# A graph layer's tiles with a second accumulator, another order of TensorE's work, and VectorE's loop over gathered pairs behind pair 2

## The reference

```python
def _graph_conv_max(x, src, dst, W_rel, b, W_root):          # N = 1250 nodes, 41250 edges, D = 512
    agg = jax.ops.segment_max(x[src], dst, num_segments=N)
    agg = jnp.where(jnp.isfinite(agg), agg, 0.0)
    return agg @ W_rel.T + b + x @ W_root.T
h = jax.nn.relu(_graph_conv_max(layernorm(x), src, dst, W1_rel, b1, W1_root))
h = jax.nn.relu(_graph_conv_max(h, src, dst, W2_rel, b2, W2_root))
x = x + h
x = x + experts(layernorm(x))                                # router, top 512 of each of 8 experts, gelu, sum
```

## Time and profile before

| | us |
|---|---|
| median of 3 runs | 1025.27 (1024.95 to 1028.95) |
| span of the profiled execution | 1025.1 |
| tiles 1 to 9 of layer 0, from end of `agg` to end of `agg` | 286.9 |
| tiles 11 to 19 of layer 1 | 297.6 |
| DVE busy in these | 212.0 and 232.7 |
| PE busy in these | 212.5 and 228.4 |

### The profile page before, as it was taken

How to read it: one execution, slowest core, us unless ns; L and a number is a source line. 1 busy time by engine, 2 the same in 40 slices (tenths; PEclk the granted TensorE clock), 3 DMA queues, 4 the chain that set the end, 5 groups by cost and what they waited for, 6 DMA issues and landing times.

```text
span 1025.1 us, 9702 instructions
## 1 busy us (share of the span) xinstructions
PE 726.0 (71%) x2541; PEld 329.5 (32%) x2541; DVE 681.6 (66%) x1232; ACT 270.3 (26%) x389; POOL 546.7 (53%) x537
## 2 busy tenths in 40 slices
PE   0317555778378778866488657887698678789996
PEld 0214222333133323322133323333243235344442
DVE  3768565588758767873888774898588879733120
ACT  0264250222022202222434030343243122012222
POOL 5652326557746675764556655566447200565644
PEclk9757877899789989987899878998899889899999
DMA  5715336557746675656657756666566400377656
GB/s 136 219 36 183 101 97 184 162 170 214 216 116 194 184 218 144 202 168 184 174 177 214 226 163 180 189 213 193 158 193 187 143 12 1 113 235 142 105 102 82
DMA packets 64770, 162.18 MB, mean 158 GB/s; under 512 B 16383, under 2 KB 20755, under 8 KB 64709
## 3 DMA queue, kind: packets, MB, share of 16 engines
q0 software_dynamic: 40448, 124.74, 44.6%
q1 hardware_dynamic: 17004, 17.16, 6.0%
q10 hardware_dynamic: 7272, 19.74, 5.9%
HBM read 143.37 MB, written 18.11 MB: 158 GB/s over the span
## 4 chain that ended last, share of the span: by engine, by line
PE 33%; DVE 25%; issue 19%; another core or an unknown queue 9%; ACT 5%; POOL 3%; DMA 2%; DVEq 2%; POOLq 0%; ACTq 0%; SPq 0%
PE pp L1165 8%; DVE acc L891 6%; PE prow L1136 5%; PE pp L1563 5%; DVE weights L902 5%; PE pp L1576 4%; PE prow L1103 3%; PE prow L1124 2%; DVE mem L1403 2%; POOL mem L838 1%; DMA mem<-tab,ic 1%; PE pp L1346 1%; PE prow L519 1%; PE pp L501 1%
## 5 line engine op out<-in xcount | busy, mean ns | idle before, releaser
L838 POOL DMA_INDIRECT mem<-tab,ic x372 | 389.5, 1047 | 266.9 <-issue 136.5
L1165 PE MATMUL pp<-weights,slots 128*128 128x512 bf16 x1200 | 306.8, 405 | 114.8 <-DVE acc L891 70.2
L891 DVE TENSOR_TENSOR acc<-acc,pp 128x1024 f32<-128x1024 f32 x180 | 219.1, 1217 | 85.3 <-PE pp L1165 33.5
L1165 PEld LDWEIGHTS pp<-weights,slots 128*128 128x128 bf16 x1200 | 118.0, 103 | 307.5 <-issue 103.8
L902 DVE TENSOR_TENSOR weights<-weights,mem 128x1024 f32<-128x1024 f32 x129 | 158.1, 1226 | 17.9 <-DVE weights L902 11.3
L1136 PE MATMUL prow<-weights,aggT 128*128 128x512 f32 x160 | 92.2, 708 | 37.4 <-ACT aggT L1213 20.5
L1124 PE MATMUL prow<-weights,rootT 128*128 128x512 f32 x160 | 76.0, 619 | 0.0
L1615 POOL DMA_INDIRECT out<-mem,node_of x28 | 44.2, 1577 | 47.3 <-ACT mem L1593 40.9
L1544 DVE COPY weights<-prow 128x512 f32<-128x512 f32 x28 | 18.7, 688 | 72.1 <-PE prow L1103 71.7
L1604 POOL DMA_INDIRECT mem<-xnd,slot_of x20 | 22.0, 1099 | 78.4 <-DVE weight_of L1538 72.6
L1213 ACT ACTIVATE aggT<-prow 128x512 f32<-128x512 f32 x20 | 11.9, 597 | 192.5 <-PE prow L1103 98.7
(11 more groups left out here) (349 smaller groups left out, 828.0 us busy)
## 6 DMA issues: line engine op xcount, KB each, us to landing
slots<-ttd ACTq DMA_DIRECT2D x20, 640.0 KB
mem<-tab,ic POOLq DMA_INDIRECT x372
...
```

Of the source, the lines that this page charges most:

```text
L838: g.indirect_dma_start(ring[:, h * PAIR + k, :], None, tables[l], bass.IndirectOffsetOnAxis(ic[:, j * PAIR + k:j * PAIR + k + 1], 0))\
L891: v.tensor_tensor(acc[:, :, :], acc[:, :, :], pp[j % 2][:, :, :], ALU.max).then_inc(S["pa"], 1)
L1165: ins = t.matmul(pp[j % 2][:, i, :], sel[u][:, j * KP + i, :], hot[:, j, w, :], start=w == 0, stop=w == 2)
```

## The change

It does four things in the 18 tiles k = 1 to 9 and 11 to 19.

1. TensorE's pairs go to one of two accumulators, `accs[k % 2]`: `acc`, or the first two thirds of `spare`, a tile that also holds what were `hst`, `x2t` and `xnT`. The wait for the last tile's `agg` goes from VectorE's start of a tile.
2. `first_two` merges the gathered pairs 0 and 1 into `accg`, `pe_first` the gathered pair 2 with TensorE's pair 0, `pool_after_first` the gathered pair 3 behind pair 1 (in the heavy tile each is one earlier). The bounds of the next tile are loaded ahead of `merge`.
3. VectorE's loop stands behind pair 2 in place of pair 5 and goes over 4 to m; pair m + 1 stays between pairs 8 and 9. The last tile's small work comes behind the loop.
4. On TensorE each half of `neighbours_product` moves behind the next pair, and `root_product` is cut in two halves around pair 6.

In tile 10 the start and the bounds of the loop change, its place doesn't. The number of instructions on operands of full size is the same.

```diff
@@ -114,8 +114,10 @@
         carry = sb("carry", [P, D])
         acc, agg = sb("acc", [P, 2, D]), sb("agg", [P, D])
         xin, rootT, aggT = sb("xin", [P, D]), sb("rootT", [P, C, P]), sb("aggT", [P, C, P])
-        hst, x2t = sb("hst", [P, D]), sb("x2t", [P, D])
-        xnT = sb("xnT", [P, C, P])
+        spare = sb("spare", [P, 3 * D])
+        hst, x2t = spare[:, 0:D], spare[:, D:2 * D]
+        xnT = spare[:, 2 * D:3 * D].rearrange("p (c m) -> p c m", c=C)
+        accs = [acc[:, :, :], spare[:, 0:2 * D].rearrange("p (a d) -> p a d", a=2)]
...
@@ -886,9 +888,10 @@
 
             def pe_pair(k, j):
 
+                m = accs[k % 2]
                 v.wait_ge(S["pairs"], k * PAIRS + (j + 1))
                 v.wait_ge(S["pa"], k * PAIRS + j)
-                v.tensor_tensor(acc[:, :, :], acc[:, :, :], pp[j % 2][:, :, :], ALU.max).then_inc(S["pa"], 1)
+                v.tensor_tensor(m, m, pp[j % 2][:, :, :], ALU.max).then_inc(S["pa"], 1)
...
-            def first_three(k, lo):
-
-                v.wait_ge(S["ready"], first_pair + lo + (FLYING + 1))
+            def first_two(k, lo):
+
+                if k % NQ == HEAVY:
+                    v.wait_ge(S["ready"], first_pair + lo + (FLYING + 1))
+                    v.scalar_tensor_tensor(accg, carry[:, :].unsqueeze(1).to_broadcast([P, 2, D]), cap[:, :],
+                                           in_ring(lo), ALU.min, ALU.max).then_inc(S["done"], 1)
+                else:
+                    v.wait_ge(S["ready"], first_pair + lo + (FLYING + 2))
+                    v.tensor_tensor(accg, in_ring(lo), in_ring(lo + 1), ALU.max).then_inc(S["done"], 2)
+
+            def pe_first(k, lo):
+
+                slot = lo + 1 if k % NQ == HEAVY else lo + 2
+                v.wait_ge(S["ready"], first_pair + slot + (FLYING + 1))
                 v.wait_ge(S["pairs"], k * PAIRS + 1)
-                v.tensor_tensor(acc[:, :, :], in_ring(lo), pp[0][:, :, :], ALU.max).then_inc(S["pa"], 1)
-                v.wait_ge(S["pa"], k * PAIRS + 1)
-                v.sem_inc(S["apart_v"], 1)
-                if k % NQ == HEAVY:
-                    v.wait_ge(S["ready"], first_pair + lo + (FLYING + 2))
-                    v.wait_ge(S["done"], first_pair + lo + SUBS)
-                    v.scalar_tensor_tensor(accg, carry[:, :].unsqueeze(1).to_broadcast([P, 2, D]), cap[:, :],
-                                           in_ring(lo + 1), ALU.min, ALU.max).then_inc(S["done"], 2)
-                    pool_pair(lo + 2)
-                else:
-                    v.wait_ge(S["ready"], first_pair + lo + (FLYING + 3))
-                    v.wait_ge(S["done"], first_pair + lo + SUBS)
-                    v.tensor_tensor(accg, in_ring(lo + 1), in_ring(lo + 2), ALU.max).then_inc(S["done"], 3)
+                v.tensor_tensor(accs[k % 2], in_ring(slot), pp[0][:, :, :], ALU.max).then_inc(S["pa"], 1)
+
+            def pool_after_first(k, lo):
+
+                slot = lo + 2 if k % NQ == HEAVY else lo + 3
+                v.wait_ge(S["ready"], first_pair + slot + (FLYING + 1))
+                v.wait_ge(S["done"], first_pair + slot + (SUBS - 1))
+                v.tensor_tensor(accg, accg, in_ring(slot), ALU.max).then_inc(S["done"], 2)
...
+                m = accs[k % 2]
                 if l:
-                    v.scalar_tensor_tensor(acc[:, :, :], accg, BIG, acc[:, :, :], ALU.min, ALU.max).then_inc(S["merge"], 1)
+                    v.scalar_tensor_tensor(m, accg, BIG, m, ALU.min, ALU.max).then_inc(S["merge"], 1)
                 else:
-                    v.tensor_tensor(acc[:, :, :], acc[:, :, :], accg, ALU.max).then_inc(S["merge"], 1)
+                    v.tensor_tensor(m, m, accg, ALU.max).then_inc(S["merge"], 1)
...
-            def vec_tile(k):
+                        cv.link(v.tensor_copy(carry[:, :], m[:, 0, :]))
+
+            def extent(q):
+
+                both = v.value_load(both1[0:1, q:q + 1], min_val=MINP // 2 - 2, max_val=NQ * LCAP // 2 * 64)
+                return v.snap(both // 64), v.snap(both % 64)
+
+            def vec_tile(k, lo, m):
                 q = k % NQ
-                both = v.value_load(both1[0:1, q:q + 1], min_val=MINP // 2 - 2, max_val=NQ * LCAP // 2 * 64)
-                lo, m = both // 64, both % 64
-                if k:
-                    v.wait_ge(S["fin"], k)
-                    v.sem_inc(S["apart_v"], 1)
                 if k == 0:
                     v.wait_ge(S["pairs"], 1)
-                    v.tensor_copy(acc[:, :, :], pp[0][:, :, :]).then_inc(S["pa"], 1)
+                    v.tensor_copy(accs[0], pp[0][:, :, :]).then_inc(S["pa"], 1)
...
-                    first_three(k, lo)
+                    first_two(k, lo)
+                    pe_first(k, lo)
...
                         pe_pair(k, j)
+                        if j == 1:
+                            pool_after_first(k, lo)
                         if j == 6:
-                            with v.Fori(3, m) as i:
+                            with v.Fori(4, m + 1) as i:
                                 pool_pair(lo + i)
-                        if j == 7:
-                            pool_pair(lo + m)
                         if j == 8:
                             pool_pair(lo + m + 1)
...
                 else:
-                    first_three(k, lo)
+                    first_two(k, lo)
+                    pe_first(k, lo)
                     pe_pair(k, 1)
+                    pool_after_first(k, lo)
                     pe_pair(k, 2)
+                    if q == HEAVY:
+                        pool_pair(lo + 3)
+                    with v.Fori(4, m + 1) as i:
+                        pool_pair(lo + i)
+                    pe_pair(k, 3)
                     if l:
                         add_and_moments(q - 1)
-                        pe_pair(k, 3)
+                        pe_pair(k, 4)
                         guess(q - 1)
                     else:
-                        pe_pair(k, 3)
-                    pe_pair(k, 4)
-                    if l == 0 and q:
-                        clamp(q - 1)
+                        pe_pair(k, 4)
+                        if q:
+                            clamp(q - 1)
                     pe_pair(k, 5)
-                    with v.Fori(3, m) as i:
-                        pool_pair(lo + i)
                     pe_pair(k, 6)
                     pe_pair(k, 7)
-                    pool_pair(lo + m)
                     pe_pair(k, 8)
                     pool_pair(lo + m + 1)
                     pe_pair(k, 9)
+                ahead = extent(q + 1) if q + 1 < NQ else None
                 v.wait_ge(S["done"], first_pair + lo + m + (SUBS + 2))
                 v.sem_inc(S["apart_v"], 1)
                 merge(k)
+                return ahead
 
...
+            bounds = extent(0)
             for q in range(NQ):
-                vec_tile(l * NQ + q)
+                bounds = vec_tile(l * NQ + q, *bounds)
...
@@ -1173,17 +1190,22 @@
                 pairs(k, (0, 1))
                 if q:
                     neighbours(k - 1)
-                    neighbours_product(k - 1, (0, 1))
                 pairs(k, (2,))
                 if q:
+                    neighbours_product(k - 1, (0, 1))
+                pairs(k, (3,))
+                if q:
                     neighbours_product(k - 1, (2, 3))
-                pairs(k, (3, 4))
+                pairs(k, (4,))
                 if k != NQ:
                     root(k)
                 pairs(k, (5,))
                 if k != NQ:
-                    root_product(k, range(C))
-                pairs(k, (6, 7, 8, 9))
+                    root_product(k, (0, 1))
+                pairs(k, (6,))
+                if k != NQ:
+                    root_product(k, (2, 3))
+                pairs(k, (7, 8, 9))
                 if l and q:
                     turn_rows(q - 1)
                     logits(q - 1)
```

7 lines of the change are left out of this document (3 added, 4 removed).

## The result

The changed kernel takes 1082.13 us (median of 4 runs, 1079.97 to 1092.78), the kernel before 1025.11 us beside it (4 runs, 1017.04 to 1028.95). The ratio is 1.059, with a 95% interval from 1.052 to 1.066. It is slower, as forecast, but by 57 us where the sum had 22, and 1082.13 lies just above the range.

What follows compares the result with a forecast made beforehand. No engine is full; handovers between TensorE and VectorE inside a destination tile bound the kernel. Ordinary tiles +12, eleven-pair tiles +4 and heavy tiles +6 make +22 on 1025.1: 1047 us, range 1008 to 1082.

Steps and rivals of the forecast that it cites:

- the sum: Whole kernel: 12 + 4 + 6 = +22 us on the profiled 1025.1, giving 1047.
- The start of a tile: VectorE's first merges: idles of 0.58 and 0.65 go, saving 1.15 us a tile; pair 2 no longer waits.
- the rival of the unsaved handover: Tile start: independent operations start no sooner than chained ones, or the bounds' load still stands; +21 us, 1068; chance 0.06.
- The 1.68: Layer 0, VectorE's wait read as for pair 2 behind half a product; claimed gone, since pair 2 comes before any product.
- The ordinary tile: Nine-pair tiles: start's savings given back in the tail, TensorE late; +1.0 and +0.45 us a tile, about +12 in all.
- Running dry: Loop waits for gathered pairs: 1.0 us in each of four eleven-pair tiles (+4); heavy tile +4 and +2 by layer.
- The clock: Heavy tile: after TensorE stands from 10.6 to 22.7, a stretch at the lower clock adds 1 to 3 us.
- Late reports: VectorE and ScalarE wait though TensorE's instruction has ended in the trace: 49 us in the 18 tiles, total taken as unchanged.
- Neither rival that lived on them: Late reports: loop hides them, 1013 us, chance 0.25; or longer gather runs make more of them, 1093 us, chance 0.12.
- The cancelled losses: Ring ahead of the loops, clock holds, ordinary tile's loss too small to place: 1025 us, no change; chance 0.10.
- the forecast's own range: Whole kernel: 1030 to 1062 us, from the terms' own bounds; forecast chance 0.47.

Runs made afterwards that it cites:

- the quiet chip: Both kernels unedited on a chip of the experiments, where the late reports are gone: before 948.07 us, changed 1003.40 us, ratio 1.065.
- the trace of the kernel before at 946.2 us: Profile of the unedited kernel before on a chip of the experiments; profiled span 946.2 us, that run measured 948.07 us.
- the halved kernels: Kernel before and changed kernel, each with one of the two gathers of each pair left out: 940.07 us (ratio 0.995) and 964.50 us (1.022).
- filling the stands: Changed kernel with unused matmuls added on TensorE before pair 5, sized to fill its stands in the loop: 998.23 us, ratio 1.057.

## Why the prediction was right in sign and wrong in size

- **The start of a tile.** Right in what it saves. On a chip without late reports 11.4 us stood at pair 0 in the 18 tiles and 1.6 do now, and the idle ahead of the first merge of gathered pairs alone goes from 21.0 (15.8 of it ended by SyncE's queue) to 5.4. That an operation that doesn't need the one before starts 1.14 us after it holds (318.57 to 319.71), and so the rival of the unsaved handover falls. The Trainium skill ("VectorE: DVE Perf Modes", section "The DRAIN you can't avoid") lets the next operation start only when the pipe is empty, but adds that one which isn't held starts earlier; the 1.14 agrees with that. The 1.68 that the prediction counted as gone at pair 2 was a wait for pair 3, as shown above.
- **The ordinary tile.** Right for nine pairs. The waits before pairs 6 and 7 should be 3.8 us in layer 0 and 2.1 in layer 1. On the quiet chip they are 2.3 + 1.8 and 0.4 + 1.8. The tiles with nine pairs should take 27.5 and 28.25; they take 27.9 and 28.2, and 28.5 and 28.9. But only four tiles have nine. Of the five with seven or eight in this class, two lose 0.4 and 0.7 and three gain 0.1 to 1.9: before, tiles 4, 7 and 14 stood 2.2, 1.4 and 3.3 us at their start for gathered pairs, and no longer do. +6.3 forecast, +1.5 measured.
- **Running dry.** This is the step that failed, with its terms of +4 and +6. The sum gave an 11-pair tile 1.0 us for it, about the middle of "index 9 lands at 13.1 to 14.4" against a want at 12.8 (by the prediction's own spacing of the turns, 6.0 + 5 x 1.41, the want is 13.05). In the tile shown above its merge starts at t = 16.6, 3.8 late and 2.2 beyond the late end of that range. The parts: pair 6 starts at 2.0 instead of 1.3, since GpSimd waits for the first merge to end and starts 0.9 behind it; eight issues take 11.7 instead of 10.4, since I took their length from outside the loop while they now stand in it; and the pair is taken 2.9 us behind the end of its last issue (334.60 to 337.49), where the range had 1.4 to 2.7. 0.7 + 1.3 + 0.2 = 2.2. The 1.4 stands in no row, and the row named for the 2.7 gives 3.0 (624.73 to 627.69). In the trace of the kernel before at 946.2 us a gather lands 3.2 us behind the start of its issue at the earliest and 3.7 in the median, some 2.2 and 2.7 behind its end. So the whole range was set too low, for the one resource that the change drains. In the heavy tiles the last turn of the loop starts at 26.1 and 24.6, where the sum had 21.5.
- **What follows a dry loop.** A late turn is paid in full, since TensorE owes five pairs and a product behind it, whatever it had time for before. Before, TensorE had its root product beside the loop and owed two pairs behind it. The tile shown lasts 35.4 us: 27.9 of a tile with nine pairs, 2.8 for two more turns, 3.8 for the late turn, and 0.9 for the clock and whatever else. So an 11-pair tile loses 5.6 to 7.9 us, not 1.7, a heavy tile 8.7 and 6.1 instead of 4 and 2; ten pairs and tile 1 (behind tile 0, whose gathered pairs are all merged last) 2.4 to 4.5, where I had seen nothing of it. By the halved kernels the gathers make 35 us of 59. My terms for it were 10.
- **The clock.** The low clock behind the stand was foreseen for the heavy tile alone (1 to 3 us). On the quiet chip it comes in all eight tiles with ten pairs or more, behind stands of 2.9 to 18.2 us; filling the stands gave 11 us back in seven of them and 5 to 7 in all.
- **Late reports.** Taken as unchanged, and the loss doesn't hang on them: it is 57 us with them and 59 without. In the first pair of traces, merges at VectorE that start over 0.4 us late by both engines' records add up to 36 us before (first merges of a tile included, less the half microsecond that they stand anyway) and 46 after. The 12.19 of the earlier trace rows comes on top before: there it was ScalarE's copy of the transposes that started 10.8 us late (275.04 to 285.88), and TensorE's product waited for it. So 49 was about right, and it hardly moved. The longest, in the changed kernel:

```profile
812.54 1.22 DVE L894 TENSOR_TENSOR acc<-acc,pp 128x1024 f32<-128x1024 f32 x1 [8.64 <-remote]
```

  Neither rival that lived on them came in: the loop hid some at pairs 2 to 4, and they stood before pairs 5 to 8 instead.
- **The cancelled losses** (no change) needed a ring ahead of the loops. It wasn't.

The direction came out right, though not by the tiles that were to carry it: those with seven to nine pairs lost 1.5 us where the sum had 6.3. The eight tiles with ten pairs or more and tile 1 lost 50.5 us where the sum had 15.4, and these 35 us are what the forecast's own range, up to 1062, left out.

What stays open: why TensorE's reports come late in the first measurement and in none of the others. And the 24 us between the halved kernels were not split further; the clock behind the stands is likely part of them, which no run shows.
